# Query, key and value projections of two query tiles as seven block products

## The chip, the cores and the metric

The kernel is one program on one core of a Trainium2 chip. The metric is the device time of one execution in microseconds (us), shown as the median of several runs. One further execution was recorded instruction by instruction; its time and its trace are what this document reads. Engines are called as in the profile: PE (matrix products), PEld (loads of its stationary operand), ACT (activations and copies), DVE (vector work), POOL (elementwise work beside DVE), SP (the queue that issues DMAs).

## What is computed

The input x has 2 sequences of 512 tokens and 512 channels. The result is a half step of a gated feed-forward network, one attention block, and the same half step again, each with a residual sum:

```python
x = x + 0.5 * ffn(layernorm(x))
x = x + attn(layernorm(x))
x = x + 0.5 * ffn(layernorm(x))
# attn: 32 query heads, 8 key/value heads, head size 128
q, k, v = xn @ Wq.T, xn @ Wk.T, xn @ Wv.T
q, k = rmsnorm(q, q_norm_w), rmsnorm(k, k_norm_w)
p = softmax(q @ k.T / sqrt(128) + causal_alibi_bias)
out = (p @ v) @ Wo.T
```

All of it is wanted at float32 quality. Every operand of a large product is therefore split in two parts, a rounded high part (written by ACT as a cast, names ending in `_h` or `_hi`) and the rest (written by POOL or DVE as a subtraction, `_l` or `_lo`), and one product is three matmuls: high by high, high by low, low by high (`matmul3`, L284 to L286).

## The kernel before

The program has three stretches: the first feed-forward step, the attention, the second feed-forward step. In the attention the outer loop runs over the 8 key/value heads (groups g, each with 4 query heads) and the inner loop over 8 query tiles of 128 tokens (4 of each sequence). One pair (g, tile) is a unit n = 0 to 63, and one **slot** of the schedule belongs to each. In a group the slots are numbered at = 0 to 7; the causal mask gives the tile number i = at mod 4 the keys of i + 1 blocks of 128, so slots with i = 0 are light and slots with i = 3 heavy.

Each engine runs an order that is written out by hand in a function `slot(n)` of its own; engines meet only at semaphores, and an engine that waits holds up all that stands behind it in its order. In slot n the engines do this:

- PE: the scores of unit n (12 matmuls); the product of probabilities and values of unit n-1 (`weigh_values`, L518 to L523); the query part of the projection of unit n+4 (`project(n + LEAD, "q")`, 12 matmuls of 512 columns); the transposes of the query and key rows of unit n+1 (`turn_rows`); the key and value part of the projection (12 matmuls of 256 columns); the output projection of unit n-1 (`project_out`, 12 matmuls of 512 columns); the transposes of the probabilities of unit n (`turn_probabilities`, L507).
- ACT: the exponentials of unit n (L822, four, one for each head); the high part of the weighed values of unit n-1 (`oT_h`, L842); the division by the sums (L831); copies of the projections out of PSUM (L795, L801, L802); `qT_h` and `kT_h`; the high parts of the transposed probabilities (L837). Weight splits are set in between: the output weights of the group (`o_h`, L790) at the ends of slots at = 0 and at = 1's probabilities, the projection weights of the next group (L782) at at = 2 and 3.
- DVE: scores plus bias with the row minimum of the negated scores (L1195), sums of squares (L1169), `oT_l` (L1212), in even slots the inverse roots of two units (`pair_roots`, eleven steps from L917 to L926), `qT_l` and `kT_l`, the residual sum (L1220), `probT_l` (L1206).
- POOL: the rows times their inverse roots (`norm_rows`, L1369), their squares (`square_rows`, L1363), and the low parts of all weights (L1294).

`project_out(n - 1)` waits for `oT_l` of unit n-1, which DVE makes from what ACT cast to `oT_h`, and the cast stands behind the exponentials of unit n in ACT's order. The sum x of all tiles stays in SBUF (`x_rows`) throughout. Eight PSUM banks rotate by least recent use.

## Time and profile before

| | |
|---|---|
| median of 3 runs | 1263.63 us (1263.17 to 1263.85) |
| the profiled execution | 1262.72 us, its span 1261.4 us |
| PE busy | 1239.9 us, 98% of the span |
| PEld busy | 1057.1 us, 84% |
| DVE busy | 802.9 us, 64% |
| ACT busy | 733.5 us, 58% |
| POOL busy | 523.8 us, 42% |

"Busy" is the time in which an engine has an instruction in work. PE's instructions overlap: the distance between the starts of two neighbours says what one costs in a stream, and is shorter than the duration shown for it. The span runs from the first instruction to the last. A bracket at the end of a row of the timeline gives the idle time before the instruction and whose result ended it.

### The profile page before, as it was taken

How to read it: one execution, taken by the hardware profiler on the slowest of the kernel's cores; microseconds unless marked ns; L12 is line 12 of the kernel's file. 1: busy time of each engine (PE TensorE's matmuls, PEld its weight loads, DVE VectorE, ACT ScalarE, POOL GpSimd, SP SyncE). 2: the span in 40 equal slices, each digit the busy share in tenths (PEclk: the TensorE clock that was granted, in tenths of full speed). 3: DMA queues.
4: the chain of work that ended last, by engine and by line, in shares of the span. 5: the costliest groups of instructions: out<-in, count | busy, mean ns of one | idle time of the engine just before them, and what ended most of it. 6: DMA issues, size and time to landing. Idle time of an engine off the chain costs nothing.

```text
span 1261.4 us, 18366 instructions
## 1 busy us (share of the span) xinstructions
PE 1239.9 (98%) x6562; PEld 1057.1 (84%) x6562; DVE 802.9 (64%) x1978; ACT 733.5 (58%) x1738; POOL 523.8 (42%) x412
## 2 busy tenths in 40 slices
PE   6999999999999999999999999999999989999999
PEld 5788888888888888888888888888888878888887
DVE  7976665766665666666566565666666777655554
ACT  4554443267667657667666666666666684544432
POOL 4686551644225224324315314313413243765550
PEclk9999999999999999999999999999999999999999
DMA  6153222101001001001101001001101010121101
GB/s 227 39 160 114 103 102 84 51 1 56 29 1 50 35 1 51 34 1 51 35 1 51 35 1 51 34 1 51 35 1 51 1 50 1 51 83 51 51 17 67
DMA packets 15018, 60.20 MB, mean 48 GB/s; under 512 B 2064, under 2 KB 2736, under 8 KB 12880
## 3 DMA queue, kind: packets, MB, share of 16 engines
q1 hardware_dynamic: 14688, 58.73, 13.4%
q8 instruction: 53, 0.87, 0.3%
q14 instruction: 37, 0.30, 0.1%
q10 hardware_dynamic: 240, 0.30, 0.1%
HBM read 45.91 MB, written 13.11 MB: 47 GB/s over the span
## 4 chain that ended last, share of the span: by engine, by line
PE 85%; ACT 5%; DVE 5%; POOL 2%; issue 1%; DMA 1%; SPq 0%; DVEq 0%; ACTq 0%; POOLq 0%
PE bank L284 19%; PE bank L285 19%; PE bank L286 19%; PE bank L507 5%; PE bank L363 4%; PE bank L369 4%; PE bank L364 4%; PE bank L518 3%; PE bank L519 3%; PE bank L523 3%; ACT prob L822 2%; PE bank L486 2%; ACT prob L831 2%; POOL o_l L1294 1%; DVE probT_l L1206 1%
## 5 line engine op out<-in xcount | busy, mean ns | idle before, releaser
L1369 POOL TENSOR_TENSOR rows<-rows,row_root_y 128x640 f32<-128x640 f32 x64 | 80.6, 1260 | 271.4 <-DVE row_root_y L926 271.4
L822 ACT ACTIVATE prob<-prob,neg_top 128x128 f32<-128x128 f32 (+3 forms) x256 | 141.5, 555 | 75.7 <-DVE neg_top L1195 75.2
L1363 POOL TENSOR_TENSOR square<-rows 128x640 f32<-128x640 f32 x64 | 80.3, 1255 | 203.1 <-ACT rows L801 203.1
L837 ACT CAST probT_h<-bank 128x512 fp32r<-128x512 f32 x160 | 84.7, 596 | 135.9 <-PE bank L507 135.9
L831 ACT ACTIVATE prob<-prob,inverse 128x128 f32<-128x128 f32 (+3 forms) x256 | 123.4, 557 | 1.8 <-DVE inverse L1200 1.8
L284 PE MATMUL bank<-w_h_late,xnT_hi 128*128 128x512 f32 (+1 forms) x352 | 121.2, 344 | 0.0
L286 PE MATMUL bank<-w_h_late,xnT_lo 128*128 128x512 f32 (+1 forms) x352 | 118.6, 337 | 0.0
L285 PE MATMUL bank<-w_l_late,xnT_hi 128*128 128x512 f32 (+1 forms) x352 | 118.3, 336 | 0.0
L1294 POOL TENSOR_TENSOR w_l_late<-raw_late,w_h_late 128x512 fp32r<-128x512 f32 (+1 forms) x58 | 88.3, 1540 | 68.3 <-ACT w_h_late L615 68.3
L1206 DVE TENSOR_TENSOR probT_l<-bank,probT_h 128x512 fp32r<-128x512 f32 x160 | 101.6, 685 | 21.9 <-ACT probT_h L837 21.8
L1195 DVE CUSTOM_DVE_ANT_0 prob<-bank,bias 128x128 f32<-128x128 f32 (+3 forms) x256 | 109.7, 485 | 0.0
L1220 DVE TENSOR_TENSOR x_rows<-bank,x_rows 128x512 f32<-128x512 f32 x64 | 44.2, 691 | 102.8 <-PE bank L286 102.8
L1182 DVE SCALAR_TENSOR_TENSOR qT_l<-bank,q_scale,qT_h 128x512 fp32r<-128x512 f32 x64 | 48.0, 751 | 95.3 <-ACT qT_h L810 95.3
L284 PE MATMUL bank<-o_h,oT_h 128*128 128x512 f32 x256 | 101.7, 397 | 4.8 <-DVE oT_l L1212 3.6
L991 DVE SCALAR_TENSOR_TENSOR x_rows<-bank,x_rows 128x512 f32<-128x512 f32 x112 | 75.7, 687 | 45.8 <-PE bank L369 45.8
L285 PE MATMUL bank<-o_l,oT_h 128*128 128x512 f32 x256 | 100.4, 392 | 0.0
L286 PE MATMUL bank<-o_h,oT_l 128*128 128x512 f32 x256 | 100.0, 390 | 0.0
L284 PE MATMUL bank<-kT_h,qT_h 128*128 128x128 f32 (+3 forms) x256 | 86.6, 338 | 1.0 <-DVE qT_l L1182 1.0
L286 PE MATMUL bank<-kT_h,qT_l 128*128 128x128 f32 (+3 forms) x256 | 82.2, 321 | 0.0
L285 PE MATMUL bank<-kT_l,qT_h 128*128 128x128 f32 (+3 forms) x256 | 82.1, 321 | 0.0
L507 PEld LDWEIGHTS bank<-ident,prob 128*128 128x128 f32 x640 | 73.7, 140 | 8.3
L507 PE MATMUL bank<-ident,prob 128*128 128x128 f32 x640 | 80.3, 272 | 0.0
(181 smaller groups left out, 3465.7 us busy)
## 6 DMA issues: line engine op xcount, KB each, us to landing
raw_late<-w_qkv SPq DMA_DIRECT2D x8, 1536.0 KB, 6.2
raw_early<-ffn_w SPq DMA_DIRECT2D x21, 512.0 KB, 4.2
scaled<-raw_early SPq DMA_DIRECT2D x21, 512.0 KB, 2.6
raw_late<-scaled SPq DMA_DIRECT2D x21, 512.0 KB, 3.6
raw_late<-w_o SPq DMA_DIRECT2D x8, 1024.0 KB, 4.8
y<-x_rows SPq DMA_DIRECT2D x8, 256.0 KB, 2.0
x_rows<-x SPq DMA_DIRECT2D x7, 256.0 KB, 5.5
...
```

The costliest lines, as they stand in the source:

```text
L284: pe.matmul(bank, lh, rh, start=first, stop=False, skip_group_check=more)
L285: pe.matmul(bank, lh, rl, start=False, stop=False, skip_group_check=more)
L286: return pe.matmul(bank, ll, rh, start=False, stop=last, skip_group_check=more)
L507: last = pe.transpose(bank[:, h * P:(h + 1) * P], prob[:, h, j * P:(j + 1) * P], ident[:, :])
L822: last = act.activation(p, p, ACT.Exp, bias=neg_top[:, h:h + 1], scale=-1.0, accum_out=total[:, h:h + 1])
L831: act.activation(p, p, ACT.Copy, scale=inverse[:, h:h + 1]).then_inc(prob_done, 1)
L837: act.copy(probT_h[:, j, :, :], banks[r.bank][:, :].rearrange("p (h q) -> p h q", h=G)).then_inc(probT_hi_done, 1)
L1195: dve.tensor_tensor_reduce(prob[:, h, 0:keys], banks[r.bank][:, 0:keys], bias[:, h, S - keys:S], -(2.0 ** -g), -MASKED, ALU.add, ALU.min, ...
L1206: dve.tensor_tensor(probT_l[:, j, :, :], banks[r.bank][:, :].rearrange("p (h q) -> p h q", h=G), probT_h[:, j, :, :].bitcast(F32), ALU.sub ...
L1294: return pool.tensor_tensor(lo, raw, hi.bitcast(F32), ALU.subtract)
L1363: pool.tensor_tensor(square[:, n % 2, :, :], row, row, ALU.mult).then_inc(squares_done, 1)
L1369: pool.tensor_tensor(row, row, by, ALU.mult).then_inc(rows_normed, 1)
```

## The change

The projections of two neighbouring query tiles are done together. Tokens (two tiles by two halves of the channels) and weights (two halves of the channels by two halves of 384 columns) are seen as 2 by 2 blocks, and the product is formed from seven block products of 384 columns instead of eight, by sums of blocks ahead of them (`s1` to `s4` of the tokens, `t1` to `t4` of the weights) and sums of products behind them. Each block product is 6 matmuls.

- From unit 16 on (`FIRST_PAIRED`) this form is used. Units 0 to 15 keep the plain form, but cut at 384 and 384 columns (`left`, `right`) instead of 512 and 256. A slot does the projection of the unit four ahead, so slots 12 to 59 work in the new form. Even slots do products 1 and 2 ahead of `turn_rows` and product 6 behind `project_out`; odd slots do 5 and 7 ahead, and 4 and 3 behind. Products 1, 6, 7 and 4 run up in one PSUM bank (bank 0, which leaves the rotation), 5 and 3 in another.
- ACT copies the running sum out after products 1, 6, 7 and 4 (`take_sum`, `take_left`), and DVE adds it to products 2, 5 and 3 (`add_products`).
- The sums of the tokens are made once, in slots 4 to 7, by POOL (`sum_tokens`, five instructions for a pair of tiles), rounded by ACT in slots 5 to 8 (`token_sums_round`) and subtracted by POOL (`token_sums_rest`).
- The sums of the weights are made by POOL for each group from 2 on (`mix_qkv`, in slots at = 3 and at = 4), and seven blocks of weights are split instead of four (`QKV_WHEN`, `QKV_REST`). The splits stand either ahead of the exponentials of a slot or at its end. The second half of the `o_h` splits at at = 1 is also ahead of the exponentials now.
- In slots from 14 on both squares of a pair are made by POOL at the start of the even slot, and both sums of squares by DVE behind `oT_l`. The low part of the values goes from DVE to POOL.
- To make room for the token sums, the running sum x lies in DRAM during the attention: it is stored once before, and each slot loads 256 KB into one of two buffers (`x_ring`) and stores 256 KB, on SP's queue.

The core of the diff:

```diff
+SEVEN_FROM = 2
+FIRST_PAIRED = SEVEN_FROM * B * TB
...
+SEVEN_QKV = {1: ("a11", "b11"), 2: ("a12", "b21"), 6: ("s2", "t2"), 5: ("s1", "t1"), 7: ("s3", "t3"), 4: ("a22", "t4"),
+             3: ("s4", "b22")}
...
+        QKV_REST = ({2: ((), ("b11", "b21")), 3: ((), ("b12", "b22"))},
+                    {2: ((), ("b11", "b21")), 4: (("t2", "t1"), ()), 5: (("t3",), ("t4", "b22"))})
+        QKV_MIX_WHEN = {3: ("t1", "t3", "t2"), 4: ("t4",)}
+        QKV_WHEN = ({2: ((), ("b11", "b21")), 3: ((), ("b12", "b22"))},
+                    {2: ((), ("b11", "b21")), 4: (("t2", "t1"), ("t3",)), 5: (("t4", "b22"), ())})
...
+            def product_qkv(n, m):
...
+                r, bank = result("seven", n, m, bank=None if m in (2, 5) else results["seven", n, 5].bank if m == 3 else 0)
+                w_h, w_l = qkv_place(g, block)
+                for k in range(2):
+                    w = slice(k * HALF, (k + 1) * HALF)
+                    last = matmul3(bank[:, 0:HALF], tokens[k], (w_h[:, w], w_l[:, w]), k == 0 and m in (1, 2, 5), k == 1, True)
...
             def slot(n):
+                ahead = n + LEAD
+                first, second = paired(ahead) and n % 2 == 0, paired(ahead) and n % 2 == 1
+                if ahead == FIRST_PAIRED:
+                    rotation[0] = range(1, BANKS)
                 scores(n)
                 if n:
                     weigh_values(n - 1)
-                if n + LEAD < UNITS:
-                    project(n + LEAD, "q")
+                if first:
+                    product_qkv(ahead, 1)
+                    product_qkv(ahead, 2)
+                elif second:
+                    product_qkv(ahead - 1, 5)
+                    product_qkv(ahead - 1, 7)
+                elif ahead < UNITS:
+                    project(ahead, "left")
                 if n + 1 < UNITS:
                     turn_rows(n + 1)
-                if n + LEAD < UNITS:
-                    project(n + LEAD, "kv")
+                if ahead < FIRST_PAIRED:
+                    project(ahead, "right")
                 if n == UNITS - 1:
                     turn_normed(2, 0)
                 if n:
                     project_out(n - 1)
+                if first:
+                    product_qkv(ahead, 6)
+                elif second:
+                    product_qkv(ahead - 1, 4)
+                    product_qkv(ahead - 1, 3)
                 turn_probabilities(n)
...
+            def token_sums_round(u):
+                act.wait_ge(x_kept, 16 * B * TB)
+                act.wait_ge(token_sums_done, 4 * (u + 1))
+                act.copy(token_sums[u][1][:, :, :], token_sums[u][0][:, :, :]).then_inc(token_sums_hi, 1)
...
+                soon_splits, late_splits = QKV_WHEN[g + 1 >= SEVEN_FROM].get(at, ((), ())) if g < HKV - 1 else ((), ())
+                if at == 1:
+                    split_o(g, (2, 3))
+                split_qkv(g + 1, *soon_splits)
+                if 0 <= n - LEAD - 1 < PAIRS:
+                    token_sums_round(n - LEAD - 1)
                 exponentials(n, range(soon))
                 if n:
                     weigh_values(n - 1)
                 exponentials(n, range(soon, G))
                 probabilities(n)
-                if at == 1:
-                    split_o(g, (2, 3))
-                if n + LEAD < UNITS:
-                    project_q(n + LEAD)
+                ahead = n + LEAD
+                if ahead < FIRST_PAIRED:
+                    project_left(ahead)
+                elif ahead < UNITS:
+                    take_sum(ahead, 1) if n % 2 == 0 else take_sum(ahead - 1, 7)
                 if n + 1 < UNITS:
                     turn_rows(n + 1)
-                if n + LEAD < UNITS:
-                    project_kv(n + LEAD)
-                elif n < UNITS - 1:
-                    split(1, 0, *(("a11", "a12"), ("a21", "a22"), ("d0", "d1"))[n + LEAD - UNITS])
-                if g < HKV - 1 and at == LEAD - 2:
-                    split_qkv(g + 1, range(AHEAD))
-                if g < HKV - 1 and at == LEAD - 1:
-                    split_qkv(g + 1, range(AHEAD, KC))
+                if n % 2 == 0 and paired(n + 2):
+                    values_hi(n + 2)
+                if ahead < FIRST_PAIRED:
+                    project_right(ahead)
+                elif ahead >= UNITS and n < UNITS - 1:
+                    split(1, 0, *(("a11", "a12"), ("a21", "a22"), ("d0", "d1"))[ahead - UNITS])
+                if paired(ahead):
+                    take_sum(ahead, 6) if n % 2 == 0 else take_left(ahead - 1)
...
+                split_qkv(g + 1, *late_splits)
...
+                if n % 2 == 0 and paired(n + 2):
+                    sum_squares(n + 2)
+                    sum_squares(n + 3)
                 if n % 2 == 0 and n + LEAD - 2 < UNITS:
                     pair_roots(n + LEAD - 2)
                 if n == UNITS - 3:
                     normal_roots(2, 0)
+                if paired(ahead):
+                    add_products(ahead, 2) if n % 2 == 0 else add_products(ahead - 1, 5)
...
+            def mix_qkv(g, *blocks):
+                for block in blocks:
...
+                    left, right = {"t1": ("b12", "b11"), "t2": ("b22", "t1"), "t3": ("b22", "b12"), "t4": ("b21", "t2")}[block]
+                    pool.tensor_tensor(qkv_raw[block], qkv_raw[left], qkv_raw[right], ALU.subtract).then_inc(qkv_mixed, 1)
...
+            def sum_tokens(u):
...
+                pool.tensor_tensor(whole_pair, xnT_hi[:, :, cols].bitcast(F32), xnT_lo[:, :, cols].bitcast(F32),
+                                   ALU.add).then_inc(whole_pair_done, 1)
+                a11, a12, a21, a22 = (whole_pair[:, k:k + 2, tile * P:(tile + 1) * P] for tile in range(2) for k in (0, 2))
+                s1, s2, s3, s4 = (token_sums[u][0][:, n, :].rearrange("p (k c) -> p k c", k=2) for n in range(4))
...
+                pool.tensor_tensor(s1, a21, a22, ALU.add).then_inc(token_sums_done, 1)
+                pool.tensor_tensor(s3, a11, a21, ALU.subtract).then_inc(token_sums_done, 1)
+                pool.wait_ge(token_sums_done, 4 * u + 1)
+                pool.tensor_tensor(s2, s1, a11, ALU.subtract).then_inc(token_sums_done, 1)
+                pool.wait_ge(token_sums_done, 4 * u + 3)
+                pool.tensor_tensor(s4, a12, s2, ALU.subtract).then_inc(token_sums_done, 1)
...
+                ahead = n + LEAD
+                soon, late = QKV_REST[g + 1 >= SEVEN_FROM].get(at, ((), ())) if g < HKV - 1 else ((), ())
+                if n % 2 == 0 and paired(n + 2):
+                    square_rows(n + 2)
+                    square_rows(n + 3)
+                split_qkv(g + 1, *soon)
                 if n + 2 < UNITS:
                     norm_rows(n + 2)
-                if n + LEAD < UNITS:
-                    square_rows(n + LEAD)
-                elif n < UNITS - 1:
+                if n % 2 == 0 and paired(n + 2):
+                    values_lo(n + 2)
+                if ahead < FIRST_PAIRED:
+                    square_rows(ahead)
+                elif ahead >= UNITS and n < UNITS - 1:
                     if n == UNITS - 3:
                         normalize(2, 0)
-                    split(1, 0, *(("a11", "a12"), ("a21", "a22"), ("d0", "d1"))[n + LEAD - UNITS])
-                if g < HKV - 1 and at == LEAD - 2:
-                    split_qkv(g + 1, range(AHEAD))
-                if g < HKV - 1 and at == LEAD - 1:
-                    split_qkv(g + 1, range(AHEAD, KC))
+                    split(1, 0, *(("a11", "a12"), ("a21", "a22"), ("d0", "d1"))[ahead - UNITS])
+                split_qkv(g + 1, *late)
+                if SEVEN_FROM <= g + 1 < HKV:
+                    mix_qkv(g + 1, *QKV_MIX_WHEN.get(at, ()))
+                if 0 <= n - LEAD - 1 < PAIRS:
+                    token_sums_rest(n - LEAD - 1)
+                if 0 <= n - LEAD < PAIRS:
+                    sum_tokens(n - LEAD)
...
+            def ring_store(n):
+                g, b, t = unit(n)
+                r = results["out", n]
+                sp.wait_ge(evac[r.bank], r.nth)
+                if g < HKV - 1:
+                    sp.dma_start(x_between[b * TB + t], x_ring[:, n % 2, :]).then_inc(ring_out[n % 2], 16)
+            def ring_load(n):
+                g, b, t = unit(n)
+                if n > 1 and unit(n - 2)[0] < HKV - 1:
+                    sp.wait_ge(ring_out[n % 2], 16 * (n // 2))
+                sp.dma_start(x_ring[:, n % 2, :], x_between[b * TB + t]).then_inc(ring_in[n % 2], 16)
```

What this does to the orders of the engines is seen at three places. The first is ACT at the end of slot 5 and in slot 6 (`sum_h` are the rounded token sums). Before:

```order
L837 CAST probT_h<-bank 128x512 x2
L822 ACTIVATE prob,total<-prob,neg_top 128x384 x4
L842 CAST oT_h<-bank 128x512
L831 ACTIVATE prob<-prob,inverse 128x384 x4
L795 COPY rows<-bank 128x512
```

Now:

```order
L978 CAST probT_h<-bank 128x512 x2
L897 CAST sum_h<-sum 128x1024
L963 ACTIVATE prob,total<-prob,neg_top 128x384 x4
L983 CAST oT_h<-bank 128x512
L972 ACTIVATE prob<-prob,inverse 128x384 x4
L910 COPY rows<-bank 128x384
```

A cast of 1024 columns of token sums stands ahead of the exponentials. What such a cast reads is made by POOL in the slot before. POOL from the end of slot 3 to slot 5, before:

```order
L1363 TENSOR_TENSOR square<-rows 128x640
L1294 TENSOR_TENSOR w_l_late<-raw_late,w_h_late 128x768 x2
L1369 TENSOR_TENSOR rows<-rows,row_root_y 128x640
L1363 TENSOR_TENSOR square<-rows 128x640
L1369 TENSOR_TENSOR rows<-rows,row_root_y 128x640
```

Now:

```order
L1588 TENSOR_TENSOR square<-rows 128x640
L1463 TENSOR_TENSOR ahead_l<-raw_late,ahead_h 128x768
L1463 TENSOR_TENSOR w_l_late<-raw_late,w_h_late 128x768
L1594 TENSOR_TENSOR rows<-rows,row_root_y 128x640
L1588 TENSOR_TENSOR square<-rows 128x640
L1550 TENSOR_TENSOR xn<-xnT_hi,xnT_lo 128x1024
L1555 TENSOR_TENSOR sum<-xn 128x256
L1556 TENSOR_TENSOR sum<-xn 128x256
L1558 TENSOR_TENSOR sum<-sum,xn 128x256
L1560 TENSOR_TENSOR sum<-xn,sum 128x256
L1594 TENSOR_TENSOR rows<-rows,row_root_y 128x640
```

Five instructions of one `sum_tokens` (`xn` is the room for the whole tokens) follow the square of the unit four ahead, in slots 4 to 7; in slots 5 to 8 a subtraction `sum_l` of 1024 columns stands between the square and them. The second place is the weights of the next group, in slots at = 4 and 5 of groups 2 to 6. POOL before, from the end of at = 3 on:

```order
L1363 TENSOR_TENSOR square<-rows 128x640
L1294 TENSOR_TENSOR w_l_late<-raw_late,w_h_late 128x768 x2
L1369 TENSOR_TENSOR rows<-rows,row_root_y 128x640
L1363 TENSOR_TENSOR square<-rows 128x640
L1369 TENSOR_TENSOR rows<-rows,row_root_y 128x640
```

POOL now (L1538 is `mix_qkv`, the one here makes `t4`; `v_l` is `values_lo`; the last three L1463 rows are the rests of `t3`, `t4` and `b22`):

```order
L1588 TENSOR_TENSOR square<-rows 128x640 x2
L1463 TENSOR_TENSOR w_l_late<-xn,w_h_late 128x768
L1463 TENSOR_TENSOR ahead_l<-xn,ahead_h 128x768
L1594 TENSOR_TENSOR rows<-rows,row_root_y 128x640
L1463 TENSOR_TENSOR v_l<-rows,v_h 128x128 x2
L1538 TENSOR_TENSOR xn<-raw_late,xn 128x768
L1463 TENSOR_TENSOR ahead_l<-raw_late,ahead_h 128x768
L1594 TENSOR_TENSOR rows<-rows,row_root_y 128x640
L1463 TENSOR_TENSOR ahead_l<-xn,ahead_h 128x768
L1463 TENSOR_TENSOR w_l_late<-raw_late,w_h_late 128x768
```

ACT from the end of slot at = 4 into slot at = 5 of the same groups, before and now:

```order
L837 CAST probT_h<-bank 128x512
L822 ACTIVATE prob,total<-prob,neg_top 128x256 x4
L842 CAST oT_h<-bank 128x512
L831 ACTIVATE prob<-prob,inverse 128x256 x4
L795 COPY rows<-bank 128x512
```

```order
L978 CAST probT_h<-bank 128x512
L892 CAST ahead_h<-raw_late 128x768
L892 CAST ahead_h<-xn 128x768
L892 CAST w_h_late<-raw_late 128x768
L963 ACTIVATE prob,total<-prob,neg_top 128x256 x4
L983 CAST oT_h<-bank 128x512
```

The casts of `t3`, `t4` and `b22` stand between the transposed probabilities of one slot and the exponentials of the next, and the one of `t4` reads what L1538 wrote. The third place is DVE in an even slot, from the inverse of the sums on. Before:

```order
L1195 ISA neg_top 128x1
L1169 TENSOR_REDUCE sums<-square 128x5
L1200 RECIPROCAL inverse<-total 128x4
L1212 TENSOR_TENSOR oT_l<-bank,oT_h 128x512
L917 TENSOR_SCALAR row_root_m<-sums 128x10
```

Now:

```order
L1344 ISA neg_top 128x1
L1349 RECIPROCAL inverse<-total 128x4
L1361 TENSOR_TENSOR oT_l<-bank,oT_h 128x512
L1318 TENSOR_REDUCE sums<-square 128x5 x2
L1066 TENSOR_SCALAR row_root_m<-sums 128x10
```

and from the last of the eleven steps of the roots on:

```order
L1075 SCALAR_TENSOR_TENSOR row_root_y<-row_root_b,row_root_y 128x10
L1380 TENSOR_TENSOR rows<-bank,rows 128x384
L1331 SCALAR_TENSOR_TENSOR qT_l<-bank,q_scale,qT_h 128x512
L1336 TENSOR_TENSOR kT_l<-bank,kT_h 128x128
L1370 TENSOR_TENSOR x_ring<-bank,x_ring 128x512
```

Both reductions come between `oT_l` and the roots, and an addition (L1380) between the roots and `qT_l`.

## Rows read from the trace of the kernel before

**Rows 1.** Windows: us, then busy time (and count) of each engine, clock, DMA

```profile
500.00:600.00 100.00, 99.83 (x576) 86.99 (x575) 61.37 (x185) 67.81 (x177) 32.12 (x24) 1.00 0.08 27
```

**Rows 2.** Timeline of PE, slot at = 5 of group 3: start, duration, instruction

```profile
618.17 0.36 PE L284 MATMUL bank<-kT_h,qT_h 128*128 128x256 f32 x1
...
620.38 0.40 PE L284 MATMUL bank<-ahead_h,xnT_hi 128*128 128x512 f32 x1
...
623.12 0.60 PE L486 MATMUL bank<-ident,rows 128*128 128x128 f32 x4
...
623.58 0.36 PE L284 MATMUL bank<-ahead_h,xnT_hi 128*128 128x256 f32 x1
...
625.10 0.40 PE L284 MATMUL bank<-o_h,oT_h 128*128 128x512 f32 x1
...
627.85 1.04 PE L507 MATMUL bank<-ident,prob 128*128 128x128 f32 x8
...
628.64 0.42 PE L284 MATMUL bank<-kT_h,qT_h 128*128 128x384 f32 x1
...
629.77 0.33 PE L284 MATMUL bank<-kT_h,qT_h 128*128 128x384 f32 x1
...
630.64 0.33 PE L286 MATMUL bank<-kT_h,qT_l 128*128 128x384 f32 x1
```

**Rows 3.** Timeline of ACT and DVE in the same slot

```profile
620.14 0.51 ACT L822 ACTIVATE prob<-prob,neg_top 128x256 f32<-128x256 f32 x1 [1.10 <-DVE neg_top L1195]
...
622.13 0.57 ACT L842 CAST oT_h<-bank 128x512 fp32r<-128x512 f32 x1
...
622.73 0.69 DVE L1212 TENSOR_TENSOR oT_l<-bank,oT_h 128x512 fp32r<-128x512 f32 x1 [0.29 <-ACT oT_h L842]
```

**Rows 4.** Timeline of PE, slot 61 (no projection in it)

```profile
1011.16 0.50 PE L284 MATMUL bank<-o_h,oT_h 128*128 128x512 f32 x1 [1.40 <-DVE oT_l L1212]
```

**Rows 5.** Timeline of ACT and PE, slot at = 1 of group 1

```profile
373.87 1.14 ACT L790 CAST o_h<-raw_late 128x512 fp32r<-128x512 f32 x2
375.07 0.51 ACT L822 ACTIVATE prob<-prob,neg_top 128x256 f32<-128x256 f32 x1
...
382.42 0.50 PE L284 MATMUL bank<-o_h,oT_h 128*128 128x512 f32 x1 [0.17 <-POOL o_l L1294]
```

**Rows 6.** Timeline of DVE and POOL, slot at = 4 of group 3 (starts at 606.17)

```profile
611.19 0.69 DVE L1212 TENSOR_TENSOR oT_l<-bank,oT_h 128x512 fp32r<-128x512 f32 x1 [0.84 <-ACT oT_h L842]
611.80 0.16 DVE L917 TENSOR_SCALAR row_root_m<-sums 128x10 f32<-128x10 f32 x1
...
613.84 0.17 DVE L926 SCALAR_TENSOR_TENSOR row_root_y<-row_root_b,row_root_y 128x10 f32<-128x10 f32 x1
614.09 1.26 POOL L1369 TENSOR_TENSOR rows<-rows,row_root_y 128x640 f32<-128x640 f32 x1 [6.96 <-DVE row_root_y L926]
...
615.18 0.28 DVE L1187 TENSOR_TENSOR kT_l<-bank,kT_h 128x128 fp32r<-128x128 f32 x1
615.61 1.25 POOL L1363 TENSOR_TENSOR square<-rows 128x640 f32<-128x640 f32 x1 [0.26 <-ACT rows L801]
```

**Rows 7.** Timeline of DVE, two reductions in a row

```profile
259.29 1.53 DVE L1169 TENSOR_REDUCE sums<-square 128x5 f32<-128x640 f32 x2
```

**Rows 8.** Groups of POOL and ACT by form: count, busy, mean ns, idle

```profile
L1294 POOL TENSOR_TENSOR ahead_l<-raw_late,ahead_h 128x768 fp32r<-128x768 f32 x10 | 18.2, 1842 | 0.0
L1336 POOL TENSOR_TENSOR mix<-xnT_hi,xnT_lo 128x1024 f32<-128x1024 f32 x4 | 9.6, 2412 | 36.4 <-DVE d_lo L984 36.4
L1294 POOL TENSOR_TENSOR fac_down<-fac_raw_down,fac_down 32x256 fp32r<-32x256 f32 x7 | 5.2, 743 | 6.2 <-ACT fac_down L589 6.2
L674 ACT CAST mix_h<-mix 128x1024 fp32r<-128x1024 f32 x8 | 8.2, 1051 | 9.0 <-DVE mix L1049 9.0
L782 ACT CAST ahead_h<-raw_late 128x768 fp32r<-128x768 f32 x10 | 7.9, 849 | 0.0
```

**Rows 9.** The page's DMA issues: count, size of one, us from issue to landing

```profile
x_rows<-x SPq DMA_DIRECT2D x7, 256.0 KB, 5.5
```

306 lines of the change are left out of this document (224 added, 82 removed).

## Prediction

> **What bounds the kernel now.** I read the windows first. In the attention, of which one stretch of 100 us stands for all, PE is busy 99.83 of 100 us, PEld 87, ACT 68, DVE 61 and POOL 32, at a granted clock of 1.00 [rows 1]. Busy time of PE overlaps, so the second view is the distance between starts [rows 2]: twelve matmuls of 512 columns take 2.74 us (623.12 less 620.38), 0.228 each; from the transposes to the output projection 1.98 us pass, of them 0.46 for the transposes and 1.52 for twelve matmuls of 256; five matmuls of 384 columns in the scores take 0.87 us (630.64 less 629.77), 0.174 each. The starts follow each other with no hole, so PE's own work sets the length of a slot: 10.47 us for this one (628.64 less 618.17).
>
> The third view is what PE would wait for if it came earlier. In this slot ACT starts the exponentials 1.97 us after the slot's start and the cast `oT_h` 1.99 us later; `oT_l` ends at 623.42, 5.25 after the start, 3.28 after the first exponential [rows 3]. PE begins `project_out` at 6.93. So there is 1.7 us of slack and no more. That this wait is real where PE has less to do is shown by slot 61, which holds no projection: PE stood 1.40 us for `oT_l` [rows 4].
>
> **What the change removes on PE.** Before, a slot's projection is 2.74 + 1.52 = 4.26 us. In the new form an even slot holds 12 + 6 and an odd slot 12 + 12 matmuls of 384 columns. With 0.173 each and 0.1 for the start behind the transposes an even slot costs 2.07 + 0.1 + 1.04 = 3.21, an odd slot 2.07 + 0.1 + 2.07 = 4.24. A pair saves 1.05 + 0.02 = 1.07 us. Slots 12 to 59 are 24 pairs: **25.7 us**. Plain slots (24 matmuls of 384) keep their cost. The price is bounded by the neighbours, 0.12 at 256 and 0.228 at 512; I take the scores' row, which is the same shape.
>
> The Trainium skill ("TensorE: Matmul & The Clock Gate", Back-to-back issue gap) gives the isolated distance as N/2.4 + 2.5 ns: 216, 162.5 and 109 for 512, 384 and 256 columns. A pair would then save 7.80 - 6.83 = 0.98 us and the whole 23.4; the rows here lie 10 to 13 ns above it at each width, so I stay with them.
>
> **What the new order adds: waits for `oT_l`.** In a new slot nothing of the projection stands between the transposes and `project_out`, in even and odd slots alike. PE reaches it 0.67 + 1.42 = 2.1 us earlier. For i = 1 that is 2.21 + 2.07 + 0.46 + 0.1 = 4.84 us after the start, where `oT_l` ends at 5.25 at best. For i = 0, 2 and 3, counted with the same distances, PE comes at 6.9, 6.2 and 7.5, and `oT_l` is there at 5.7 [rows 6], 6.0 and 6.7 (two blocks and three more of keys add some 0.1 us per exponential and block).
>
> *At = 1.* The casts of `o_h` stand ahead of the exponentials, four instead of two. Two took 1.20 us to the next instruction, 1.14 busy [rows 5], so four take 2.24: the exponentials start at 3.0, `oT_l` ends at 6.28, PE waits 6.34 - 4.84 = 1.5 us. In groups 2 to 7: **+9.0**. What goes in exchange is the wait for `o_l`, the last head of which held PE (0.17 idle and a restart, some 0.45 in all [rows 5]) because `o_h` of heads 2 and 3 came late: eight groups, **-3.6**.
>
> *At = 5, the casts of `t4` and `b22`.* `t4` is made by POOL at the end of slot at = 4, behind `norm_rows`, which waits for the roots. Before, the roots start 5.63 after the slot's start and end 2.21 later; `norm_rows` starts at 7.92 and takes 1.26 [rows 6]. Two reductions in a row take 1.53 us [rows 7] and now stand between `oT_l` and the roots, so the roots end at 9.4 and `norm_rows` at 10.7. Two `v_l` of 128 columns follow. No row has that; between 256 columns at 743 ns and 768 at 1842 [rows 8] the line gives 0.47 each, to 11.6. `t4` itself, 768 columns, 1.84: 13.45. The slot is 10.95 long (12.00 - 1.05), so ACT gets `t4` 2.5 us into slot at = 5. Two casts of 768, 0.85 each [rows 8] and overlapping by 0.1, let the exponentials start at 4.1 instead of 1.97. `oT_l` ends at 7.4, PE waits 7.45 - 4.84 = 2.6 us. Behind it all of the slot is late, nothing makes up for it, since PE has no hole elsewhere. Groups 2 to 6: 13.0. In group 1 the reductions still have their old place, and the wait is 1.6, with 0.7 in its slot 12, where `t2` comes behind a square: 2.3. Together **+15.3**.
>
> *Slots 5 to 8, the token sums.* POOL's square ends 10.69 after the start of slot 4 (615.61 + 1.25 less 606.17 [rows 6]). Then the whole tokens, 2.41, and four sums of 256 columns at 0.74 less overlaps [rows 8], 5.3 in all: 16.0, and slot 4 is 12.0 long. So ACT, which has the cast `sum_h` ahead of the exponentials, stands until 4.0 us into slot 5, casts for 1.05, and `oT_l` ends 3.28 later, at 8.4. Here the plain form holds and PE comes at 6.93: 1.5 us of wait. The next job is chained to this one: key rows are copied some 5.8 us (slot 6: 6.6, slot 7: 7.5) after the first exponential, an estimate from four exponentials at 0.50, four divisions alike, and the copies. Then come a square of 1.25, a rest `sum_l` of 2.4 and the sums of 5.3 again. The next slots' casts are released 7.75, 8.4 and 7.9 us after their starts; `oT_l` ends at 12.5, 13.6 and 11.9 against PE's 8.3, 9.6 and 8.9. Waits 4.2, 4.0 and 3.1, with slot 5 **+12.8**.
>
> *Slot 60* has no projection, and both reductions now stand ahead of its roots, `qT_l` and `kT_l`. Between 0 and 1.53 [rows 7]; nothing on PE covers it there, I take **+1.3**.
>
> **What I cost at nothing.** In even slots DVE's chain grows by 1.53 and an addition of 384 columns (0.5, which fits into the idle time between the roots and `kT_l`, where only `qT_l` stood). `kT_l`, which ended 9.29 after the start (615.18 + 0.28), ends at 10.8 for i = 0 and 11.05 for i = 2; the next scores start at 10.95 and 11.2. The cover is 0.1 us; if an instruction takes 0.2 more, each of 24 even slots pays, some 2 to 7 us. ACT has six copies for a pair as before, and POOL has 32% of its time in use [rows 1]. The ring of x needs a store and a load of 256 KB; even at 5.5 us each [rows 9] they land 11 us after the sum, and the buffer is wanted two slots, some 22 us, later. Bank 0 leaves the rotation, the seven others come round with their readers done.
>
> **The sum** against the profiled execution: 1262.7 - 25.7 + 9.0 - 3.6 + 15.3 + 12.8 + 1.3 = **1271.8 us**. The median of the runs is 0.9 above the profiled one, so I forecast a median of **1272.7 us**, 0.7% slower. This measurement can tell about 0.2% (2.5 us) from no change.
>
> **The rivals.** *First, POOL's results come in time* (faster). If neither `t4` nor the token sums hold ACT, 28.1 us of waits go: 1244.6. The page speaks for it with POOL at 42% and the windows with 32. Against it, both waits come from order, a wait for one result behind a wait for another, which a free engine does not shorten. Chance 0.08. If one of the two is absent, 1257 or 1260: 0.10. It would take POOL instructions of half the rows' length.
>
> *Second, the waits are half of mine*, for instance because ACT's chain behind a late release is shorter and the token jobs do not pile up: -14, or about 1259 to 1266, no difference to be told. It decides at 8 us less than my sum of waits. Chance 0.06.
>
> *Third, DVE becomes the bound of even slots* (slower still). Its chain from the slot's start to `kT_l` is 11.05 against 11.2. With 0.3 us more, reductions that don't overlap and the waits of roots among them, 24 slots give 7 us: 1280. Chance 0.10, from the thin cover.
>
> *The forecast* has 0.66, with a range of its own of 1266 to 1280: the waits rest on chained durations, each of the nine long waits uncertain by some 0.5 us, and the price of 384 columns by 1.
>
> **How the numbers follow.** Faster by over 0.2%: 0.08 + 0.10, less a little at the border, 0.17. Within 0.2%: 0.06 and the edge of the forecast, 0.08. Slower: 0.75. The range leaves the full gain and the far side of the third rival out, 1259 to 1281.
>
> **What the changed profile would show.** Right, if slots 12 to 59 in even places are about 11.0 and 11.2 us; if PE's waits are headed by `oT_l` at the output projection, 1.5 us at at = 1 and 2.6 at at = 5; if ACT waits 2 us or more for L1538 ahead of L892 in six groups, and for POOL's L1560 in slots 5 to 8, for up to 7 us each. Wrong, if ACT's waits for POOL are under 1 us there, if PE waits at the scores for `kT_l` in even slots, or if DVE waits for the ring's DMA.

## The result, and the profile after

The changed kernel takes **1273.03 us** in the median of four runs (1272.3 to 1273.74), the kernel before 1263.55 us (1263.17 to 1263.85). The ratio is 1.0075, 95% interval 1.0058 to 1.0093: slower by 0.75%. The forecast was 1272.7. The profiled execution took 1273.51 us.

The head of the page after, first the busy times, then the rows of PE and of its clock in 40 slices of 32 us:

```profile
span 1272.2 us, 18593 instructions
PE 1224.3 (96%) x6418; PEld 1068.7 (84%) x6418; DVE 826.3 (65%) x2002; ACT 753.3 (59%) x1760; POOL 649.7 (51%) x526
PE   6999999999899999999999999999999999999999
...
PEclk9999999999989999999999999999999999999999
```

PE has less to do than before and is busy for a smaller share of a longer span. Besides the first slice one shows it at 8, and one shows its clock at 8. The window that answers to [rows 1]:

```profile
500.00:600.00 100.00, 96.91 (x554) 87.61 (x553) 66.88 (x195) 71.17 (x181) 48.09 (x39) 1.00 0.20 69
```

PE, which never stood still in this stretch before, now stands for 3.1 of 100 us, at the same clock of 1.00. From 260 to 1045 us (the attention), PE's waits for `oT_l` and for a rest of the weights, and ACT's waits for POOL's sums (us in total, times, longest):

```profile
PE bank L347 <- DVE oT_l L1361: 25.7, 20, 3.9
PE bank L347 <- POOL ahead_l L1463: 4.2, 6, 0.8
ACT sum_h L897 <- POOL sum L1560: 21.0, 4, 6.8
ACT ahead_h L892 <- POOL xn L1538: 4.0, 5, 0.8
ACT w_h_late L892 <- POOL xn L1538: 2.0, 1, 2.0
```

**Slot by slot.** A slot lasts from the first matmul of its scores to that of the next slot's. Taken so from the timelines of PE in both profiled executions, in us, with "at" the place in the group:

| slots | before | after | difference, all of them |
|---|---|---|---|
| even, 12 to 58 (24) | 12.00 and 12.26 | 11.03 and 11.24 | -23.3 (slot 12 gave only 0.34) |
| at = 3 and 7, 15 to 59 (12) | 14.00 | 14.07 | +0.9 |
| at = 1, groups 0 and 1 | 10.79, 10.92 | 10.47, 10.50 | -0.7 |
| at = 1, groups 2 to 7 (6) | 10.92 | 11.93 | +6.0 |
| at = 5, groups 2 to 6 (5) | 10.47 | 12.95 | +12.4 |
| slot 13 | 10.47 | 12.07 | +1.6 |
| slots 5, 6, 7, 8 | 10.47, 12.26, 13.99, 12.01 | 12.16, 18.10, 18.00, 13.10 | +12.6 |
| slot 60 | 8.99 | 10.45 | +1.5 |
| others | | | +0.2 |

The sum is +11.2 us, against 10.8 between the two spans.

**Slots 5 to 8.** ACT's casts of the token sums and PE's output projections, timeline of the kernel after; slots 5 to 9 start at 323.99, 336.15, 354.25, 372.25 and 385.35:

```profile
328.23 1.05 ACT L897 CAST sum_h<-sum 128x1024 fp32r<-128x1024 f32 x1 [3.36 <-POOL sum L1560]
332.50 0.50 PE L347 MATMUL bank<-o_h,oT_h 128*128 128x512 f32 x1 [1.39 <-DVE oT_l L1361]
343.86 1.05 ACT L897 CAST sum_h<-sum 128x1024 fp32r<-128x1024 f32 x1 [6.79 <-POOL sum L1560]
348.56 0.50 PE L347 MATMUL bank<-o_h,oT_h 128*128 128x512 f32 x1 [3.92 <-DVE oT_l L1361]
361.01 1.05 ACT L897 CAST sum_h<-sum 128x1024 fp32r<-128x1024 f32 x1 [5.78 <-POOL sum L1560]
366.14 0.50 PE L347 MATMUL bank<-o_h,oT_h 128*128 128x512 f32 x1 [2.07 <-DVE oT_l L1361]
378.32 1.05 ACT L897 CAST sum_h<-sum 128x1024 fp32r<-128x1024 f32 x1 [5.04 <-POOL sum L1560]
382.16 0.50 PE L347 MATMUL bank<-o_h,oT_h 128*128 128x512 f32 x1 [0.84 <-DVE oT_l L1361]
```

The bracket is the idle time of the engine and what ended it. Each time ACT stands for POOL's last sum, and PE stands later for `oT_l`, the last link of what ACT has behind that cast. The longest wait has a consequence of its own. PE's matmuls right behind it, and the windows around both long waits:

```profile
349.37 0.39 PE L347 MATMUL bank<-o_h,oT_h 128*128 128x512 f32 x1
...
350.17 0.63 PE L347 MATMUL bank<-o_h,oT_h 128*128 128x512 f32 x1
350.60 0.63 PE L348 MATMUL bank<-o_l,oT_h 128*128 128x512 f32 x1
```

```profile
346.00:350.00 4.00, 1.44 (x6) 1.22 (x7) 2.13 (x10) 4.00 (x12) 0.00 (x0) 0.99 0.00 2
350.00:354.00 4.00, 4.00 (x16) 3.21 (x16) 2.37 (x8) 1.69 (x6) 3.29 (x3) 0.58 0.00 0
354.00:358.00 4.00, 4.00 (x21) 3.34 (x20) 3.72 (x10) 1.23 (x3) 3.92 (x3) 1.00 0.37 131
...
366.00:370.00 4.00, 3.86 (x11) 3.09 (x12) 1.23 (x4) 3.35 (x8) 0.73 (x1) 0.62 0.00 0
```

Up to 350 the starts stand some 0.23 apart, and from 350.17 on 0.43: the clock has fallen from its upper level (2.4 GHz) to the lower (1.2 GHz), 1.6 us after PE started again, and it is back at 1.00 by 354. The same follows the wait of 2.07 us in slot 7.

How the loss divides over these slots belongs to this one execution, the sum does not. Three kernels of the experiments below (`t4` mixed early, `oT_h` behind the first exponential, one more reduction) have the same order in slots 5 to 8. Their slots 6, 7 and 8 take 18.7 to 18.9, 15.5 to 15.8 and 14.7 us, and all four together 61.4, as here.

**At = 5**, slot 21, which starts at 530.53, ACT, POOL and PE of the kernel after:

```profile
531.29 0.84 ACT L892 CAST ahead_h<-raw_late 128x768 fp32r<-128x768 f32 x1
532.86 1.83 POOL L1463 TENSOR_TENSOR ahead_l<-raw_late,ahead_h 128x768 fp32r<-128x768 f32 x1
532.93 0.84 ACT L892 CAST ahead_h<-xn 128x768 fp32r<-128x768 f32 x1 [0.81 <-POOL xn L1538]
534.41 0.50 ACT L963 ACTIVATE prob<-prob,neg_top 128x256 f32<-128x256 f32 x1
534.74 0.45 PE L347 MATMUL bank<-ahead_h,sum_h 128*128 128x384 f32 x1 [0.80 <-POOL ahead_l L1463]
536.98 0.69 DVE L1361 TENSOR_TENSOR oT_l<-bank,oT_h 128x512 fp32r<-128x512 f32 x1 [0.29 <-ACT oT_h L983]
537.73 0.50 PE L347 MATMUL bank<-o_h,oT_h 128*128 128x512 f32 x1 [1.12 <-DVE oT_l L1361]
```

ACT casts `t3` first, then stands 0.81 us for `t4`, and starts the exponentials 3.88 us into the slot. PE is held twice: 0.80 us ahead of product 7, whose block is `t3`, because POOL works at the mix of `t4` before it comes to the rest of `t3`; and 1.12 us ahead of the output projection.

### The profile page after: what moved, and what is told of

Its sections match the earlier page's. It is cut to its first block, busy times and chain, and to the rows that moved or that the text cites. A ratio compares the mean times of both kernels' runs of the same rounds, so it can differ in the third digit from the quotient of the medians.

```text
span 1272.2 us, 18593 instructions
## 1 busy us (share of the span) xinstructions
PE 1224.3 (96%) x6418; PEld 1068.7 (84%) x6418; DVE 826.3 (65%) x2002; ACT 753.3 (59%) x1760; POOL 649.7 (51%) x526
## 4 chain that ended last, share of the span: by engine, by line
PE 75%; ACT 7%; DVE 7%; POOL 6%; issue 4%; DMA 1%; SPq 0%; ACTq 0%; POOLq 0%; DVEq 0%
PE bank L347 17%; PE bank L349 17%; PE bank L348 17%; PE bank L592 4%; PE bank L426 4%; PE bank L432 4%; PE bank L427 4%; ACT prob L963 3%; PE bank L606 2%; PE bank L607 2%; PE bank L611 2%; PE bank L571 1%; ACT o_h L905 1%; POOL xn L1538 1%; POOL rows L1594 1%
## 5 line engine op out<-in xcount | busy, mean ns | idle before, releaser
L347 PE MATMUL bank<-o_h,oT_h 128*128 128x512 f32 x256 | 106.8, 417 | 25.7 <-DVE oT_l L1361 25.7
L1463 POOL TENSOR_TENSOR w_l_late<-raw_late,w_h_late 128x512 fp32r<-128x512 f32 (+1 forms) x59 | 90.5, 1549 | 77.3 <-ACT w_h_late L720 67.9
L1380 DVE TENSOR_TENSOR rows<-bank,rows 128x384 f32<-128x384 f32 x72 | 40.0, 556 | 74.3 <-ACT rows L927 41.0
L347 PEld LDWEIGHTS bank<-o_h,oT_h 128*128 128x128 f32 x256 | 48.6, 190 | 39.2 <-DVE oT_l L1361 30.9
L1349 DVE RECIPROCAL inverse<-total 128x4 f32<-128x4 f32 x64 | 11.4, 178 | 98.0 <-ACT prob L963 98.0
L1463 POOL TENSOR_TENSOR w_l_early<-raw_early,w_h_early 128x512 fp32r<-128x512 f32 x37 | 49.5, 1355 | 41.9 <-ACT w_h_early L720 41.8
L606 PE MATMUL bank<-probT_h,v_h 128*128 128x512 f32 x160 | 63.6, 398 | 0.0
```

Of the source, the lines that this page charges most:

```text
L347: pe.matmul(bank, lh, rh, start=first, stop=False, skip_group_check=more)
L606: pe.matmul(bank[:, :], v_h[:, b, j, :], turned[2 * j], start=j == 0, stop=False)
L1463: return pool.tensor_tensor(lo, raw, hi.bitcast(F32), ALU.subtract)
```

## Experiments

Each was timed against the kernel before on the same chip as itself: 1262.84 us for the first four, 1262.52 us for the others. Differences of slots are to the profiled execution of the changed kernel unless said otherwise. The expectations write TensorE for PE, ScalarE for ACT, VectorE for DVE and GpSimd for POOL; B and C in two of them are the two terms at at = 1, +9.0 and -3.6.

### The token sums' casts at the end of the slot

```
                 split_qkv(g + 1, *soon_splits)
-                if 0 <= n - LEAD - 1 < PAIRS:
-                    token_sums_round(n - LEAD - 1)
                 exponentials(n, range(soon))
...
                 split_qkv(g + 1, *late_splits)
+                if 0 <= n - LEAD - 1 < PAIRS:
+                    token_sums_round(n - LEAD - 1)
... (GpSimd)
-                if 0 <= n - LEAD - 1 < PAIRS:
-                    token_sums_rest(n - LEAD - 1)
+                if 0 <= n - LEAD - 2 < PAIRS:
+                    token_sums_rest(n - LEAD - 2)
```

> The changed kernel with the casts of the token sums moved on ScalarE from ahead of the exponentials of slots 5 to 8 to the end of the same slots, and their rests on GpSimd one slot later. Theory: the 12.6 us that slots 5 to 8 lost are ScalarE's waits for GpSimd's sums ahead of the exponentials, so all of it comes back: these four slots within 0.5 us each of the kernel before, median 1260.5 us (1259.5 to 1262), and the granted clock shows no 0.61 stretch at 350 us. Rival: GpSimd's own load in these slots (some 8 us of sums beside the squares and norms) is what delays the rows that TensorE transposes; then the slots stay over 3 us longer in sum than before, and the median is 1264 or more. Second rival: the clock fall is set by something other than the idle stretch, and stays.

Measured: **1261.51 us** (1261.28 to 1264.21), ratio 0.9991 to the kernel before, interval 0.9982 to 0.9999. Slots 5 to 8 take 10.52, 12.32, 14.04 and 12.10 us: 12.4 of their 12.6 come back, and 0.3 appears in slot 9. The granted clock of the whole execution is 1.0. The cast that stood at 328.23 with 3.36 us of wait ahead of it now comes behind all that ACT does for slot 5 and waits for nothing:

```profile
335.18 1.07 ACT L897 CAST sum_h<-sum 128x1024 fp32r<-128x1024 f32 x1
```

POOL does the same work, its rests one slot later. So its load costs next to nothing there (0.3 us); what cost was the place of one cast on ACT. The clock's fall went with the waits.

### `t4` mixed ahead of the row norms

```
                 split_qkv(g + 1, *soon)
+                mixes_now = QKV_MIX_WHEN.get(at, ()) if SEVEN_FROM <= g + 1 < HKV else ()
+                if at == 4:
+                    mix_qkv(g + 1, *mixes_now)
                 if n + 2 < UNITS:
                     norm_rows(n + 2)
...
-                if SEVEN_FROM <= g + 1 < HKV:
-                    mix_qkv(g + 1, *QKV_MIX_WHEN.get(at, ()))
+                if at != 4:
+                    mix_qkv(g + 1, *mixes_now)
```

> The changed kernel with the weight mix t4 of GpSimd moved ahead of the row norms in the fifth slot of a group, straight behind the rests of t2 and t1. Theory: in the sixth slot ScalarE's cast of t4 ahead of the exponentials then waits for nothing, so the exponentials start 0.8 to 0.9 us earlier (3.0 to 3.1 us into the slot in place of 3.9), and five to six slots of 12.95 us become 12.1: median 1268.5 us (1267.5 to 1270). Rival: most of that slot's 2.5 us is the casts themselves and what stands behind them, not the wait: less than 2 us in all. Second rival: the norms that come 1.8 us later delay the transposes of the rows; then the fifth slots grow and nothing is won.

Measured: **1269.38 us** (1269.19 to 1272.03), ratio 1.0053, interval 1.0041 to 1.0066. The slots at = 5 fall from 12.95 to 12.03 in groups 2 to 6 (-4.6 in all) and slot 13 from 12.07 to 11.04, while slot 12 grows by 1.0. Slot 21 of this kernel starts at 530.96:

```profile
533.93 0.50 ACT L963 ACTIVATE prob<-prob,neg_top 128x256 f32<-128x256 f32 x1
...
534.54 0.45 PE L347 MATMUL bank<-ahead_h,sum_h 128*128 128x384 f32 x1 [0.17 <-POOL ahead_l L1463]
...
537.24 0.50 PE L347 MATMUL bank<-o_h,oT_h 128*128 128x512 f32 x1 [0.84 <-DVE oT_l L1361]
```

The exponentials start 2.97 us into the slot, 0.91 earlier, and the slots are 0.92 shorter in the mean. Of PE's two waits the one for the rest of `t3` gives 0.63 and the one for `oT_l` 0.28, since POOL no longer has `t4` in front of that rest. The two waits are in line: what the first gives, the second may take.

Slot 12 looks like the second rival, but its cause is another. Here the moved mix runs while DVE comes to the roots:

```profile
430.16 1.84 POOL L1538 TENSOR_TENSOR xn<-raw_late,xn 128x768 f32<-128x768 f32 x1
430.27 1.77 DVE L1068 TENSOR_SCALAR row_root_y<-row_root_m 128x10 int32<-128x10 int32 x1
```

This step of the roots takes 1.77 us, where it takes 0.17 in the changed kernel (at 429.84), and it ends 0.03 us after the mix. The roots and `qT_l` come late by it, POOL waits 1.96 us for the roots ahead of `norm_rows`, and PE stands 0.76 us at the scores of slot 13 for `qT_l`. So the roots were late before the norms were. That the mix held up this step is read from one coincidence in time, in this one place; no run tested it.

### `oT_h` behind the first exponential

```
+        def oT_first(n):
+            return unit(n)[2] == 1 and paired(n + LEAD - 1)
... (ScalarE)
+                if oT_first(n):
+                    soon = 1
                 exponentials(n, range(soon))
... (VectorE)
-                late = n + LEAD >= UNITS
+                late = n + LEAD >= UNITS or oT_first(n)
```

> The changed kernel with ScalarE's cast oT_h behind the first exponential in place of the fourth, and VectorE's oT_l ahead of the reciprocal, in the second and sixth slots of the groups whose projections are products (12 slots). Theory: the output projection of those slots waits for oT_l alone, 1.4 us at the second slot and 2.4 at the sixth; oT_l then ends at about 4.8 and 5.9 us into the slot in place of 6.1 and 7.1, so 1.2 to 1.4 us come back in each: median 1258 us (1256 to 1261). Rival: the exponentials that come behind the cast end 0.6 us later, and the probabilities' transposes or the next scores wait for them instead; then less than half of it, 1266 us or more.

Measured: **1261.13 us** in the median, but from 1258.51 to 1262.57, ratio 0.9983, interval 0.9975 to 0.9992; 3 us more than forecast and 0.1 beyond the range. The profiled execution is the fastest, the one of 1258.51. Its slots give a little less than the 1.2 to 1.4 each of the forecast: at = 1 falls from 11.93 to 10.78 (1.15 each), at = 5 from 12.95 to 11.84 (1.11 each), slot 13 by 1.1, -13.6 in all, and slots 5 to 8 take 61.4 together as before. Another 1.4 us of its lead lies ahead of slot 5, where the edit changes nothing. In slot 17 of this kernel, which starts at 479.83:

```profile
483.18 0.57 ACT L986 CAST oT_h<-bank 128x512 fp32r<-128x512 f32 x1
...
483.79 0.69 DVE L1366 TENSOR_TENSOR oT_l<-bank,oT_h 128x512 fp32r<-128x512 f32 x1 [0.99 <-ACT oT_h L986]
...
484.59 0.47 PE L350 MATMUL bank<-o_h,oT_h 128*128 128x512 f32 x1
...
487.10 0.46 ACT L930 COPY rows<-bank 128x384 f32<-128x384 f32 x1
...
487.61 0.44 PE L350 MATMUL bank<-ahead_h,xnT_hi 128*128 128x384 f32 x1
```

`oT_l` ends 4.65 us into the slot, and PE, which comes at 4.76, does not wait for it. But a smaller wait takes its place, as the rival had it in kind and not in size. ACT ends the copy of the running sum (L930) 7.73 us into the slot, 0.37 later than in the changed kernel, and product 4, which runs up in the same bank, starts behind it, at 487.61: 0.40 us after the start before it, where 0.23 is usual, and 0.28 ahead of the next, where 0.17 is usual. That is 0.3 us in each slot at = 1, which without any wait would take some 10.5 and not 10.78. Why the other runs of this kernel are up to 4 us longer stays open.

### The kernel before, with the output weights' casts ahead of the exponentials

```
                 soon = G if unit(n)[2] == 0 or n + LEAD < UNITS else G // 2 if unit(n)[2] == 1 else G - 1
+                if at == 1:
+                    split_o(g, (2, 3))
                 exponentials(n, range(soon))
...
-                if at == 1:
-                    split_o(g, (2, 3))
                 if n + LEAD < UNITS:
                     project_q(n + LEAD)
```

> The kernel before with ScalarE's last two casts of the output weights moved from behind the probabilities to ahead of the exponentials in the second slot of each group, as the change does it, and nothing else. Theory (terms B and C of the prediction): TensorE's wait for o_l of 0.45 us goes eight times, -3.6 us, and the two casts put the exponentials off by 1.5 us, which ends oT_l at about 4.8 us into the slot, where the longer projection of this kernel ends as well: no new wait. Median 1260 us (1259 to 1261). Rival: oT_l is late here too, and the move brings nothing or costs, 1263 us or more.

Measured: **1259.24 us** (1259.1 to 1259.65), ratio 0.9969, interval 0.9957 to 0.9981. Every slot at = 1 that was 10.8 to 10.9 us long is now 10.47; no other slot moves by more than 0.04. The move alone is a gain of 3.6 us where PE has the longer projection as cover.

### The same casts put back in the changed kernel

The edit is that of the last experiment, undone: `split_o(g, (2, 3))` stands behind `probabilities(n)` again.

> The changed kernel with ScalarE's casts of the third and fourth part of the output weights put back behind the probabilities in the second slot of each group, where the kernel before has them. Theory: the exponentials of these slots start 1.1 to 1.5 us earlier, but the output projection now comes at 5.3 us into the slot and waits for o_l, whose two rests on GpSimd end near 8.0 and 9.2 us: 1.0 us longer than with the move in six slots, and 0.45 us longer in two: 1279.5 us (1277 to 1281). So terms B and C are what one must pay here. Rival: with the shorter products the 1.5 us that the move costs outweigh the late o_l, and the kernel gets faster by 3 us or more, 1270 or less.

Measured: **1281.34 us** (1280.67 to 1281.94), ratio 1.0149, interval 1.0135 to 1.0163; 0.3 above the range that was expected. At = 1 in groups 2 to 7 takes 12.97 in place of 11.93 (+6.2 in all), in groups 0 and 1 0.4 more each. Slots 5 to 8 take 1.6 more, which was not foreseen: PE's clock falls in slot 8 too, as told in the last section. Slot 17, which starts at 484.33:

```profile
489.62 0.50 PE L347 MATMUL bank<-o_h,oT_h 128*128 128x512 f32 x1 [0.29 <-DVE oT_l L1361]
...
492.37 0.50 PE L347 MATMUL bank<-o_h,oT_h 128*128 128x512 f32 x1 [1.11 <-POOL o_l L1463]
```

The wait for `oT_l` is nearly gone, and two for `o_l` take its place, this one and one of 0.28 at 493.61. The early casts are the lesser of two waits, by 1.0 us a slot.

### One more reduction in the even slots

```
                 if n % 2 == 0 and paired(n + 2):
                     sum_squares(n + 2)
                     sum_squares(n + 3)
+                    dve.tensor_reduce(more_sums[:, n // 2, :], square[:, (n + 3) % 2, :, :], AX.X, ALU.add)
```

> The changed kernel with one more reduction of 0.74 us on VectorE (its result goes to a spare tile) ahead of the roots in each of the 24 even slots that have two already. It measures how much room VectorE's chain has left there, which decided between my forecast (no cost) and the third rival (0.3 us each): kT_l ends 10.74 and 10.99 us into these slots, and the next scores start at 11.03 and 11.24, so 0.25 to 0.3 us are free and the rest shows: +0.45 to +0.55 us in each of 24 slots, 1284 us (1282.5 to 1286). If VectorE's chain is not what TensorE meets next, under +3 us in all; if the reductions cost more than their own length, over +18.

Measured: **1282.9 us** (1282.07 to 1283.77), ratio 1.0162, interval 1.0148 to 1.0176. The edit acts in the even slots 14 to 60. The 23 of them up to 58 take 11.43 and 11.69 in place of 11.03 and 11.24, +9.7 in all, and slot 60 another 0.6. In slot 22 of this kernel (545.09 to 556.79):

```profile
552.42 0.81 DVE L1406 TENSOR_REDUCE more_sums<-square 128x5 f32<-128x640 f32 x1
...
556.40 0.28 DVE L1337 TENSOR_TENSOR kT_l<-bank,kT_h 128x128 fp32r<-128x128 f32 x1
```

`kT_l` ends 11.59 us into the slot, 0.60 later than in the changed kernel (10.99), and the slot is 0.45 longer. So 0.15 to 0.2 us are free there, a little less than I read off the ends of `kT_l`. Part is given back: in the slots at = 1, ACT works at its casts while PE is late, and they take 11.53 in place of 11.93 (-2.4); the slots at = 5 take 0.2 more each.

### Idle time of PE in five lengths

The kernel before, with small copies on ACT ahead of the exponentials; it computes the same.

```
+                if at == 6 and 2 <= g <= 6:
+                    for k in range((0, 8, 18, 30, 44)[g - 2], (8, 18, 30, 44, 61)[g - 2]):
+                        if k:
+                            act.wait_ge(spare_done, k)
+                        act.copy(spare_copy[:, :], bias[:, 0, 0:2 * P]).then_inc(spare_done, 1)
```

> The kernel before with ScalarE kept busy ahead of the exponentials of the seventh slot in groups 2 to 6, by 8, 10, 12, 14 and 17 small copies of about 0.5 us (to a spare tile). It asks at what length of TensorE's idle time ahead of the output projection its clock falls, as it did in slot 6 of the changed kernel after 3.9 us. oT_l has 2.3 us of room there, so I expect idle times of about 0.3, 1.3, 2.3, 3.3 and 4.8 us. Theory: the fall comes with the length of the idle time, so the first three keep the granted clock at 1.00 and spacings of 0.228 us, and the last or the last two show a stretch near 0.5 to 0.6 with spacings of 0.43, each costing some 1.6 us more than its idle time. Rival: the fall in slot 6 came from what went before it (the DMA writes, slot 5's own wait), and no step here shows it.

Measured: 1273.42 us in its one run. The five slots take 12.26, 12.95, 13.79, 16.25 and 17.34 us against 12.26, with these waits of PE ahead of the output projection (the first has none):

```profile
636.97 0.50 PE L286 MATMUL bank<-o_h,oT_h 128*128 128x512 f32 x1 [0.39 <-DVE oT_l L1219]
736.44 0.50 PE L286 MATMUL bank<-o_h,oT_h 128*128 128x512 f32 x1 [1.26 <-DVE oT_l L1219]
836.75 0.54 PE L286 MATMUL bank<-o_h,oT_h 128*128 128x512 f32 x1 [2.14 <-DVE oT_l L1219]
837.09 0.63 PE L287 MATMUL bank<-o_l,oT_h 128*128 128x512 f32 x1
...
939.91 0.80 PE L286 MATMUL bank<-o_h,oT_h 128*128 128x512 f32 x1 [3.45 <-DVE oT_l L1219]
```

```profile
838.00:840.00 2.00, 2.00 (x6) 1.59 (x5) 1.59 (x8) 1.53 (x6) 1.10 (x1) 0.50 0.00 0
```

### All moves together

The three moves above, `t4` only from the fourth group on, and one for slot 60:

```
                 scores(n)
                 ahead = n + LEAD
+                if n == UNITS - 4:
+                    sum_squares(n + 2)
+                    sum_squares(n + 3)
...
-                if n % 2 == 0 and paired(n + 2):
+                if n % 2 == 0 and paired(n + 2) and n != UNITS - 4:
```

> The changed kernel with all moves together: token sums cast late, t4 mixed ahead of the row norms (but not for the third group, where that lengthened slot 12 by 1.0 us), oT_h behind the first exponential in the twelve slots, and in slot 60 VectorE's two reductions ahead of its waits for ScalarE. Theory: the losses C, D, E and F are separate waits on separate slots, so their returns add: -11.5 for the tokens, six slots of 11.93 to 10.78, five of 12.95 to about 11.0 (both moves act there), slot 13 by 1.1, slot 60 by 1.3; 1272.8 - 31 = 1242 us (1240 to 1245), which is faster than the kernel before by 1.6% and bears out the prediction's first rival as what the products are worth without the waits. Rival: removed waits come back elsewhere (the transposes of the probabilities or the next scores), and the sum falls short by over a third: 1253 or more.

Measured: **1241.67 us** (1240.78 to 1242.9), ratio 0.9836 to the kernel before, interval 0.9822 to 0.9849. Against the changed kernel's slots: 5 to 8 -12.4, at = 1 -6.9, at = 5 -10.0, slot 13 -1.1, slot 60 -1.5. The returns add, but for 0.3 us that comes back in slot 9. What is left of waits is small: 0.3 us in each slot at = 1, as in the kernel with `oT_h` early, and 0.5 in each at = 5, where PE still comes before the rest of `t3` (slot 21, which starts at 516.03):

```profile
519.61 0.44 PE L350 MATMUL bank<-ahead_h,sum_h 128*128 128x384 f32 x1 [0.17 <-POOL ahead_l L1471]
```

The stretch of [rows 1] once more:

```profile
500.00:600.00 100.00, 99.82 (x580) 90.61 (x579) 68.10 (x195) 71.61 (x182) 52.70 (x43) 1.00 0.22 73
```

PE stands for 0.2 us again, and 580 matmuls fit where 576 were, narrower ones. Not all of the 1.6% is the products' doing. The kernel before gets 0.3% by moving the output weights' casts alone (1259.24 against 1262.84). Of the 20.9 us some 17, or 1.3%, are left for the products with the waits out, an estimate from the two ratios 0.9836 and 0.9969.

## Why the prediction was right, and where it was off

The mechanism was right in the main: the products save, and waits behind ACT's order cost more than they save. That the median came out 0.3 us from the forecast is luck. From profiled execution to profiled execution it is +10.8, where the sum had +9.1; the forecast then added 0.9 for the median, which after the change lies 0.5 below the profiled one. So a sum 1.7 too small met an addition 1.4 too large. Term by term:

**The saving** (-25.7). The even slots are 11.03 and 11.24, where the text said 11.0 and 11.2. They gave 0.98 to 1.03 each rather than 1.05; slot 12 gave 0.34, but the rest of it was taken by ACT's wait of 2.0 us for `t2`, which the text had booked under at = 5. The odd slots at = 3 and 7 lost 0.07 each rather than gaining 0.02. That makes 23.3 + 0.6 - 0.9 = 23.0: the term was 2.7 us too large, and this is most of what the sum missed.

**At = 1** (+9.0 and -3.6). PE came to the output projection 4.76 us into the slot (4.84 reckoned) and started it at 6.17 (6.34 reckoned). The idle time shown is only 1.17, as it counts from the end of the last transpose; the starts stand 1.45 apart, where 0.03 is usual. The six slots and the two of groups 0 and 1 together show +5.3 against a forecast of +5.4. The two experiments on `o_h` show what the move is worth: 0.45 us a slot in the kernel before, and 1.0 in the changed one, in spite of the wait of 1.2 that it brings there.

**At = 5** (+15.3). Measured +12.4 and +1.6, with 0.7 in slot 12: 14.7. The chain was right at its head: `t4` was cast 2.40 us into the slot (forecast 2.5), and the exponentials began at 3.88 (4.1). But the step "ACT gets `t4` 2.5 us into slot, PE waits 7.45 - 4.84 = 2.6" put everything on `oT_l`. PE was held first for the rest of `t3`, which cost 1.1 us with the slower start behind it, and then 1.4 for `oT_l`. Two waits in line gave the sum that one had been reckoned to give; the experiment with `t4` shows them shifting against each other. For the same reason "ACT waits 2 us or more for L1538 in six groups" was wrong: it waited 0.81 in five, as it was busy with `t3` until 1.6, and 2.0 in one. By the prediction's own list, waits under 1 us there were a sign of being wrong, and in five groups of six this sign came.

**Slots 5 to 8** (+12.8). Measured +12.6, but by slots 1.7, 5.8, 4.0 and 1.1 instead of 1.5, 4.2, 4.0 and 3.1. The chain of token jobs was right. From one cast of token sums to the next 15.6, 17.2 and 17.3 us passed, where the text's steps give 15.8, 16.6 and 17.5. (By these steps the release in slot 7 comes at 7.9 and not at 8.4, a slip of 0.5.) What was missing is the clock: behind the wait of slot 6 PE ran at the lower level, which made that slot some 1.6 us longer than its waits account for. But the casts did not move for it. In the changed kernel and in the four experiments that keep them in place they start 4.2, 19.9, 37.0 and 54.3 us after the start of slot 5, whatever PE's clock does. So the time that PE loses in slot 6 shortens its next waits (2.07 and 0.84 us here, instead of 4.0 and 3.1), and the sum stays. Only in the last of these slots is there no later wait to take it up: the kernel with the casts put back falls in slot 8, and its four slots take 63.0 and not 61.4. That the 4.0 of slot 7 came out as forecast is luck of this execution; in the four other kernels the slot loses 1.2 to 1.8. With the casts moved, 12.4 us returned at once.

**Slot 60** (+1.3): measured 1.46, and gone when the reductions stood ahead of the wait.

**At nothing.** The even slots' DVE chain was costed at nothing on a cover of 0.1 us. `kT_l` ends at 10.74 and 10.99 (reckoned 10.8 and 11.05), and the added reduction shows a true cover of 0.15 to 0.2 us. DVE waited for no DMA of the ring; on the page a load lands 2.6 us after its issue in the median.

**The rivals.** The first (1244.6 without the waits of POOL's results) did not happen in the changed kernel, but its mechanism was sound: taking those waits out, and `oT_l`'s at = 1 and 5 and slot 60 as well, gives 1241.67. Its price for POOL's results alone, 28.1, was not seen: the two experiments on them gave 12.4 and 4.6 us by their slots, and most of the rest came with `oT_h`. Its argument against itself held too, as POOL was free enough and the order was not. The second asked for waits 8 us below the sum; the two terms it spoke of came to 27.3 against 28.1. The third stayed away by 0.15 us. It was argued that "nothing makes up" for a late slot, "since PE has no hole elsewhere", and that held, but for 0.4 us in the slots at = 1 of the kernel with one more reduction.
